# One core, a post-norm decoder layer: hand-written order lists for every engine from the last self-attention group to the first up products, key blocks zeroed by DMA, a new order of the start

## The reference, cut to what matters

```
x = layernorm(x + self_attention(x))      # 16 heads, low-rank q (384) and kv (128) latents, RMS norm, rope, causal
x = layernorm(x + cross_attention(x, ctx))# 16 heads of 32, keys and values from a 128-wide latent, causal
x = layernorm(x + ffn(x))                 # 2 shared experts (4096 hidden in all) and top 2 of 16 routed experts

q_c  = rms_norm(x @ wq_down.T) * q_norm_w ;  kv_c = rms_norm(x @ wkv_down.T) * kv_norm_w
k_rope = rope(x @ wk_rope.T)   # one rope key for all heads
scores = (q_nope k_nope + q_pe k_rope) / sqrt(192), causal; softmax; out = probs @ v ; out @ wo.T
```

## Time and profile before

| | |
|---|---|
| median of 3 runs | 903.31 us (902.88 to 906.53) |
| the profiled execution | 902.72 us, its span 900.9 us |
| PE busy | 838.2 us (93%) |
| PE weight loads busy | 710.2 us (79%) |
| DVE, ACT, POOL busy | 528.1, 474.8, 240.8 us |
| mean granted clock of PE | 0.988 |
| start up to the loop | 0 to 84.4 us |
| self-attention loop, 3 rounds | 84.4 to 301.1 us, 72.2 us a round |
| last self-attention group and the way into cross-attention | 301.1 to 391.5 us |
| cross-attention loop, 3 rounds | 391.5 to 489.3 us, 32.6 us a round |
| last cross-attention group and first up products | 489.3 to 521.5 us |
| feed-forward | 521.5 to 900.9 us |

### The profile page before, as it was taken

How to read it: one execution, slowest core, us unless ns; L and a number is a source line. 1 busy time by engine, 2 the same in 40 slices (tenths; PEclk the granted TensorE clock), 3 DMA queues, 4 the chain that set the end, 5 groups by cost and what they waited for, 6 DMA issues and landing times.

```text
span 900.9 us, 13299 instructions
## 1 busy us (share of the span) xinstructions
PE 838.2 (93%) x4302; PEld 710.2 (79%) x4302; DVE 528.1 (59%) x979; ACT 474.8 (53%) x1225; POOL 240.8 (27%) x278
## 2 busy tenths in 40 slices
PE   6978999999999987889998789999999999999997
PEld 5766888788788775777776678888888988889896
DVE  3553753654664557666767755636465665656467
ACT  5514752743753554676576651525473745637150
POOL 0222230132132021455455100431232332321420
PEclk9989999999999998999999999999999999999999
DMA  8022315133322400321222020543464564653432
GB/s 324 1 78 63 123 43 157 65 99 98 123 85 55 146 21 21 84 49 38 55 52 67 2 71 24 183 166 119 146 206 164 187 199 153 198 166 131 137 94 82
DMA packets 39486, 96.33 MB, mean 107 GB/s; under 512 B 15824, under 2 KB 21840, under 8 KB 37808
## 3 DMA queue, kind: packets, MB, share of 16 engines
q1 hardware_dynamic: 28384, 57.95, 20.6%
q0 software_dynamic: 11056, 37.79, 12.9%
HBM read 71.59 MB, written 20.97 MB: 103 GB/s over the span
## 4 chain that ended last, share of the span: by engine, by line
PE 62%; issue 15%; DVE 8%; ACT 7%; POOL 4%; SPq 1%; DMA 1%; POOLq 0%; ACTq 0%; DVEq 0%
PE ps L1490 50%; ACT Pt L829 3%; PE ps L1505 3%; PE ps L1830 2%; POOL Pt L593 2%; PE ps L1820 1%; PE ps L1550 1%; PE ps L1640 1%; DVE negmax L1101 1%; SPq L514 1%; DVE acc L1117 1%; PE ps L1711 1%; PE ps L1832 1%; DVE kb L1218 1%; DVE stats L1123 1%
## 5 line engine op out<-in xcount | busy, mean ns | idle before, releaser
L593 POOL TENSOR_TENSOR Pt<-Pt,rowinv 112x448 f32<-112x448 f32 x64 | 59.9, 936 | 226.6 <-DVE rowinv L1108 226.2
L829 ACT ACTIVATE Pt<-ps,negmax 112x112 f32<-112x112 f32 x256 | 87.2, 356 | 49.1 <-DVE negmax L1101 49.0
L1490 PE MATMUL ps<-x2T_hi,ws_hi 128*128 128x448 f32 x256 | 96.0, 375 | 4.3 <-DVE x2T_lo L1030 4.3
L1490 PE MATMUL ps<-x2T_lo,ws_hi 128*128 128x448 f32 x256 | 94.2, 368 | 0.0
L1490 PE MATMUL ps<-x2T_hi,ws_lo 128*128 128x448 f32 x256 | 94.1, 368 | 0.0
L1490 PE MATMUL ps<-w_hi,h_hi 128*128 128x512 f32 x224 | 89.9, 401 | 0.0
L957 ACT ACTIVATE hf<-ps,b 128x448 f32<-128x448 f32 x64 | 40.6, 635 | 92.3 <-PE ps L1490 72.9
L1490 PE MATMUL ps<-w_hi,h_lo 128*128 128x512 f32 x224 | 88.5, 395 | 0.0
L1490 PE MATMUL ps<-w_lo,h_hi 128*128 128x512 f32 x224 | 88.4, 395 | 0.0
L1030 DVE TENSOR_TENSOR h_lo<-hf,h_hi 128x448 fp32r<-128x448 f32 x64 | 39.9, 623 | 48.7 <-ACT h_hi L958 47.9
L1374 DVE TENSOR_TENSOR acc<-ps,acc 128x512 f32<-128x512 f32 x56 | 38.6, 689 | 44.4 <-PE ps L1490 35.4
(11 more groups left out here) (282 smaller groups left out, 2248.6 us busy)
## 6 DMA issues: line engine op xcount, KB each, us to landing
stage<-in_wf SPq DMA_DIRECT2D x30, 513.0 KB
rows_in<-in_zeros SPq DMA_DIRECT2D x30, 256.0 KB, 4.0
xs<-rows_in POOLq DMA_DIRECT2D x29, 256.0 KB, 4.3
rows_out<-yb POOLq DMA_DIRECT2D x29, 256.0 KB
stage<-in_wa SPq DMA_DIRECT2D x4, 1408.0 KB, 6.6
stage<-in_wb SPq DMA_DIRECT2D x4, 1280.0 KB, 5.6
qr<-ro_hi SPq DMA_DIRECT2D x64, 56.0 KB, 2.0
qr<-ro_lo SPq DMA_DIRECT2D x64, 56.0 KB, 2.0
```

The source lines that it names most:

```text
L593: nc.gpsimd.tensor_tensor(p, p, rowinv[0:S, b % 2, :].unsqueeze(2).broadcast_to([S, GH, S]), ALU.mult).then_inc(norm_done, 1)
L829: last = nc.scalar.activation(Pt[0:S, b % 2, h * S:(h + 1) * S], ps[0:S, b % 2, h * S:(h + 1) * S], ACT.Exp, bias=negmax[0:S, b % 2, h:h + 1],
L1490: ins = mm(dst, w, x, start=start and i == 0, stop=stop and i == len(ops) - 1, skip_group_check=not (start and stop))
```

## The change

1. The start. ACT loads the table for `Sqrt` before the data are there, and the additions of epsilon on DVE are gone (they are the bias of the square root). PE's first products over the first slice of features go in the order in which their parts arrive. The turned latents, the rope keys and the first `A`, `E`, `O` items are interleaved: PE does the first half's rope keys, then `A 0`, `A 1`, `E 0`, `O 0` in banks 2, 3, 0 and 1, then the second half's latents. The first `wa_lo` is made by DVE instead of POOL, and the rope keys are added and split by POOL instead of DVE and ACT.
2. `att_ready` and `x_ready` are gone; each of the first two bank users of a loop waits for its own bank.
3. The last self-attention group, the start, loop and last list of cross-attention are written item by item for each engine. `V 0` moves behind the first `Q`, one layer norm row moves from ACT to DVE, two of the four first splits of feed-forward weights (`F 2`, `F 3`) move on POOL from the start of cross-attention to its last group.
4. `kb` is zeroed by four transfers of 128x4x448 from a zeroed row `kz` instead of four DVE memsets; in the cross-attention loop SP spreads the first half's keys before it waits for the second part of the weights.

The diff, cut to its core:

```diff
-ROWS_ON_DVE = [2, 3]
+ROWS_ON_DVE = [2, 3, 6]
+ATT_PRE = _lat0 + [("KR", 0), ("A", 0), ("A", 1), ("E", 0), ("O", 0)] + _lat1 + [
+    ("KR", 1), ("A", 2), ("E", 1), ("O", 1), ("Q", 0, 0)] + _q
+ATT_PRE_DVE = _lat0 + [("RMS", 1), ("KR", 0), ("NAT", 1), ("A", 0), ("A", 1), ("E", 0), ("O", 0)] + _lat1 + [
+    ("KR", 1)] + _kvn + [("A", 2), ("E", 1), ("O", 1), ("Q", 0, 0)] + _q
+ATT_LAST_PE = [
...
+    ("W", 0), ("Z", 2), ("S", 4), ("T", 3), ("G", 6), ("W", 1), ("Z", 3), ("T", 4), ("G", 7), ("S", 5), ("S", 6),
+    ("Z", 4), ("W", 2), ("T", 5), ("W", 3), ("S", 7), ("Z", 5), ("T", 6), ("K", 0), ("Z", 6), ("W", 4), ("T", 7),
+    ("W", 5), ("Z", 7), ("U1", 0), ("U1", 1), ("U1", 2), ("U1", 3), ("W", 6)]
+X_PRE_PE = [
+    ("U1", 4), ("Q", 0), ("V", 0), ("U1", 5), ("S", 0), ("S", 1), ("U1", 6), ("K", 1), ("V", 1), ("S", 2), ("T", 0),
+    ("Q", 1), ("S", 3), ("T", 1), ("Z", 0), ("S", 4), ("T", 2)]
+X_PE = [
+    ("Z", 1), ("S", 5), ("T", 3), ("S", 6), ("Z", 2), (NEXT, "K", 0), ("Z", 3), ("T", 4), (NEXT, "Q", 0), ("S", 7),
+    ("T", 5), (NEXT, "V", 0), (NEXT, "S", 0), ("W", 0), ("Z", 4), ("Z", 5), ("W", 1), ("T", 6), (NEXT, "K", 1),
+    (NEXT, "S", 1), ("T", 7), (NEXT, "Q", 1), (NEXT, "S", 2), ("Z", 6), ("Z", 7), ("W", 2), (NEXT, "T", 0),
+    (NEXT, "S", 3), (NEXT, "T", 1), ("W", 3), (NEXT, "V", 1), (NEXT, "S", 4), ("W", 4), (NEXT, "Z", 0),
+    (NEXT, "T", 2), ("W", 5), ("W", 6)]
+X_LAST_PE = [
+    ("Z", 1), ("T", 3), ("S", 5), ("S", 6), ("Z", 2), ("T", 4), ("Z", 3), ("S", 7), ("W", 0), ("T", 5), ("Z", 4),
+    ("T", 6), ("Z", 5), ("W", 1), ("W", 2), ("W", 3), ("Z", 6), ("T", 7), ("Z", 7), ("U2", 0), ("U2", 1), ("U2", 2),
+    ("U2", 3), ("W", 4), ("W", 5), ("FF", 0), ("W", 6), ("FF", 1), ("FF", 2), ("FF", 3), ("U2", 4), ("U2", 5),
+    ("U2", 6)]
...
-            sp.wait_ge(kb_zero, 2)
+            sp.wait_ge(kz_set, 1)
+            sp.wait_ge(a_free["G"], NG * B)
+            for half in range(2):
+                for a in range(2):
+                    sp.dma_start(f32(kb[:, half, a, :, :, :]).rearrange("p b h s -> p b (h s)"),
+                                 f32(kz[:, :]).unsqueeze(1).broadcast_to([P, HB, GH * S])).then_inc(kb_zero[half], 16)
+            sp.wait_ge(kb_zero[0], 32)
             spread_keys(0, 0)
...
                 load_x(g, 0, X_O, xl_ld)
+                spread_keys(g, 0)
                 sp.wait_ge(xo_lo, g)
                 load_x(g, X_O, X_SIZE, xo_ld)
-                spread_keys(g, 0)
                 spread_keys(g, 1)
...
-            for i, (lo, hi) in enumerate(A_PIECES):
-                pool.wait_ge(a_hi, i + 1)
-                nc.gpsimd.tensor_tensor(wa_lo[:, lo:hi], stage[:, lo:hi], f32(wa_hi[:, lo:hi]),
-                                        ALU.subtract).then_inc(a_lo, 1)
...
+                elif kind == "KR":
+                    cols = slice(j * HALF, (j + 1) * HALF)
+                    rot = rope_keys[j]
+                    pool.wait_ge(kr_mul, j + 1)
+                    nc.gpsimd.tensor_tensor(rot[:, 0, :], rot[:, 0, :], rot[:, 1, :], ALU.add).then_inc(kr_rot, 1)
+                    pool.wait_ge(kr_rot, j + 1)
+                    nc.gpsimd.tensor_tensor(kr_hi[:, cols], rot[:, 0, :], one[:, :].broadcast_to([P, HALF]),
+                                            ALU.mult).then_inc(krh, 1)
+                    pool.wait_ge(krh, j + 1)
+                    nc.gpsimd.tensor_tensor(kr_lo[:, cols], rot[:, 0, :], f32(kr_hi[:, cols]), ALU.subtract)\
+                      .then_inc(krl, 1)
...
-            act.wait_ge(one_set, 1)
+            act.wait_ge(one_set, 3)
+            nc.scalar.activation(warm[:, :], one[:, :], ACT.Sqrt)
...
+            for i, (arrived, n) in enumerate(((in_hi, 2), (in_lo, 1), (in_lo, 2))):
+                pe.wait_ge(arrived, n)
+                for b in range(HB):
+                    mm(ps[0:S, b, :], *down_terms(b, 0)[i], start=i == 0, stop=False, skip_group_check=True)
```

More of the change, by code:

```diff
@@ L183 @@
[L183 to L191, removed]
@@ L238, in count, with first_after @@
         return self.per[item[0]] * g + self.rank[item] + 1
+    def first_after(self, places, item):
+        n = places.index(item)
+        return None if n > 1 else [i for m, i in enumerate(self.pre if places is self.body else self.last)
+                                   if m % 2 == n][-1]
     def base(self, g):
@@ L246, in place @@
         n = places.index(item)
-        if n >= 2:
+        if places is self.pre and item in PRE_BANK:
+            return Place(PRE_BANK[item] - 6, number + n, None, None)
+        if n >= 2 and places[n - 2] not in PRE_BANK:
             dg, prev = group_of(places[n - 2])
@@ L258, with turns @@
 Place = namedtuple("Place", "bank number prev prev_count")
-AJ = Jobs(0, ATT_PRE, ATT_PE, ATT_LAST_PE, "AEOQGBWKV")
+AJ = Jobs(0, ATT_PRE, ATT_PE, ATT_LAST_PE, "AEOQGBWK")
 XJ = Jobs(AJ.end, X_PRE_PE, X_PE, X_LAST_PE, "QKVW", X_DONE)
-def turns(fori, jobs, pre, body, last, step, between=None):
+def turns(fori, jobs, pre, body, last, step):
     def run(order, places, g, number):
@@ L773, in _, with squares @@
             copy(maskb[0:S, :], maskf[0:S, :]).then_inc(const_done, 1)
-            for r in range(2):
+            def squares(r):
                 for b in range(HB * r, HB * r + HB):
@@ L934, in x_step @@
                     turned(0, j, x1T_hi)
[L935 to L938 removed]
+                elif kind == "EXP":
+                    function_ready(ACT.Exp)
                 elif kind == "ROOT2":
@@ L1065, in _, with values @@
                     ins.then_inc(nat_done, 1)
-                for b in range(HB * r, HB * r + HB):
-                    dve.wait_ge(kvn_hi, b + 1)
-                    low(kvN_lo[0:S, b, :], nat[0:S, b % 4, QR:QR + LAT], kvN_hi[0:S, b, :])\
-                        .then_inc(kvn_lo, 1)
-                    dve.wait_ge(tr_hi, b + 1)
-                    cols = slice(b * S, (b + 1) * S)
-                    low(qkT_lo[:, :, cols], ps[:, b, 0:4 * S].rearrange("p (c s) -> p c s", c=4),
-                        qkT_hi[:, :, cols]).then_inc(tr_lo, 1)
+            def values(b):
+                dve.wait_ge(kvn_hi, b + 1)
+                low(kvN_lo[0:S, b, :], nat[0:S, b % 4, QR:QR + LAT], kvN_hi[0:S, b, :]).then_inc(kvn_lo, 1)
+            rms(0)
+            latents(0)
+            for i, (lo, hi) in enumerate(A_PIECES):
+                dve.wait_ge(a_hi, i + 1)
+                low(wa_lo[:, lo:hi], stage[:, lo:hi], wa_hi[:, lo:hi]).then_inc(a_lo, 1)
+            for b in range(HB):
+                values(b)
             def table(i):
@@ L1185, in att_step @@
                     ins.then_inc(a_free[kind], 1)
+                elif kind == "LAT":
+                    dve.wait_ge(tr_hi, j + 1)
+                    cols = slice(j * S, (j + 1) * S)
+                    low(qkT_lo[:, :, cols], ps[:, j, 0:4 * S].rearrange("p (c s) -> p c s", c=4),
+                        qkT_hi[:, :, cols]).then_inc(tr_lo, 1)
+                elif kind == "RMS":
+                    rms(j)
+                elif kind == "NAT":
+                    latents(j)
+                elif kind == "VAL":
+                    values(j)
+                elif kind == "KR":
+                    for s in range(2):
+                        dve.wait_ge(kr_done, 2 * j + s + 1)
+                        ins = nc.vector.tensor_tensor(batches(rope_keys[j][:, s, :]),
+                                                      batches(ps[:, 2 * j + s, 0:HALF]), table(2 + s), ALU.mult)
+                    ins.then_inc(kr_mul, 1)
                 elif kind == "SA":
@@ L1530, in _ @@
                         .then_inc(kr_done, 1)
-                if half == 0:
-                    for b in range(HB, B):
-                        turn_latents(b)
-            pe.wait_ge(tr_lo, B)
             def heads(ap):
```

250 lines of the change are left out of this document (129 added, 121 removed), and 43 rows, old and new, of tables (ATT_LAST_ACT, ATT_LAST_DVE, ATT_LAST_PE, X_LAST_ACT).

## The result

The changed kernel takes 858.75 us (median of 4 runs, 856.66 to 860.35) against 903.10 for the kernel before (4 runs, 902.07 to 906.53). The ratio is 0.9501, 95% interval 0.9469 to 0.9534. The forecast was 865 us, 850 to 881. The profiled execution took 858.94 us with a span of 857.1, so 43.8 us of span are gone. PE's idle time in the span fell from 62.7 to 30.1 us, and its busy time from 838.2 to 827.0 us with the same 4302 matmuls; the mean granted clock rose from 0.988 to 0.996.

A forecast was written before the change was run, and what follows sets the result against it. PE, busiest in every stage, was taken to bound the kernel, losing time idle or at the lower clock. Gains of 13.5 + 10.5 + 1.0 + 8.4 + 4.5 + 0.2 = 38.1 us off 902.72 gave 864.6, stated as 865, range 850 to 881.

The forecast's parts named there:

- the start: Start, up to the self-attention loop: waits and lower-clock time go, 13.5 us gained, between 10 and 16.
- the last group: Last cross-attention group: feed-forward products and W items cover layer norm and splits, 4.5 of 9.5 us gained, between 2 and 7.
- signs of being wrong: PE waiting for kb, kvN_lo taking 1 us or more with PE behind it, or second-loop rounds above 31.5 us.
- (f): Start: POOL's rope keys beside DVE's kvN_lo take 2 us of DVE and PE time away, bounds 0 and 3.5.
- (a): Start: table loaded before the data and PE beginning with hi*hi, 2.0 us gained, bounds 1.3 and 2.1.
- (d): Start: Q 1 1 no longer has to be split before the loop starts, 1.7 us gained.
- The last self-attention group: Last self-attention group: transfers replace DVE memsets and items are reordered, 10.5 us gained, between 7 and 14.
- The cross-attention loop: Cross-attention loop: new lists cover the small waits, 2.8 us a round, 8.4 in three, between 1.0 and 4.6 a round.
- slower than before: Rival: S 0 waits for keys in every cross-attention round and the clock falls, 908 us; chance 0.04.
- The way in: Stretch between self-attention and the cross-attention loop: half of its 2.0 us idle time kept, 1.0 us gained.
- Waits that only move: Rival: no gain in the cross-attention loop and half the last self-attention group's gain lost, 878 us; chance 0.22.
- All gaps closed: Rival: all PE idle time after its first matmul and the clock loss go, 54 us, 849; chance 0.13.

The follow-up runs named there:

- e11: Changed kernel without the early load of ACT's table, new order of first products kept; 858.75 us, ratio 0.9526.
- e10: Changed kernel with the four zeroing transfers of the key blocks issued three times over, each set after the last landed; 876.53 us, ratio 0.9718.
- e3: Changed kernel with the key blocks zeroed by four DVE memsets again and the zeroing transfers dropped; 866.64 us, ratio 0.9611.
- e2: Changed kernel, but in the cross-attention loop SP again spreads the first half's keys after waiting for the second part of the weights; 882.02 us, ratio 0.9782.
- e4: Changed kernel with U2 4 to U2 6 ahead of FF 3 on PE and ahead of FF 2 on ACT; 857.23 us, ratio 0.9508.
- e7: e4 with the gate's copies and first split of down weights taken out of FF 1 and put behind U2 on ACT and DVE; 853.14 us, ratio 0.9465.
- e8: e7 with W 4 ahead of Z 7 on PE, Z 5 ahead of SQRT on ACT, last self-attention group's W 0 behind Z 2 and S 4; 852.28 us.
- e12: e8 with SB 1 and G 1 swapped on ACT in self-attention; 852.73 us, ratio 0.9457.
- e6: The changed kernel itself, run again beside the kernel before; 858.01 us, ratio 0.9519.
- e9: Changed kernel with rope keys added and their low part made by DVE, high part copied by ACT, instead of POOL; 860.98 us, ratio 0.9554.

## Why the prediction was right, and where a size was off

**The mechanism and the sign** held: PE lost time in five stages, idle or at the lower clock level, and the new order takes most of it back; 43.8 us are gone where 38.1 were forecast. 32.6 of them are idle time. The terms did not all hold: the start passed its upper bound of 16 by 0.2, and the last group, by the estimate below, fell short of its lower bound of 2. One of the prediction's own signs of being wrong came in small: a `kvN_lo` took 1.25 us and PE waited 0.6 us behind it.

**The start.** The walk was right (`G 0` at 64.8 us, predicted 64.6; PE's first product at 5.0, predicted 4.8; granted clock 1.00). The sum was below it by the 2.0 us for DVE and POOL blocking each other (f). The blocking is real (`kvN_lo` 2.60 us for 0.9), but DVE was waiting for PE on both sides of it, and PE waited 0.6 for what DVE made next. The table's part of (a) is 1.0 to 1.5 us at the loop (e11), too little to be told in the whole time. (d), 1.7 us, was counted as gone: 1.1 of it moved into the first loop round. With the 1.5 us that the self-attention loop took longer, 14.7 us are left of the 16.2, nearer to the forecast than the row of the start shows.

**The last self-attention group.** 11.5 for 10.5; the waits found by the walk (0.6 us at `Z 6`) were there at 0.7. The price of the zeroing transfers was too high: 16 us taken from the earlier trace rows, 11.7 measured (e10), in both cases hidden. What I did not say is what the memsets would cost under the new lists: 8.3 us (e3). Without the transfers 2.6 us of that stage's gain are left.

**The cross-attention loop** is the term that was mis-sized most: 2.8 us a round taken, 4.1 measured, a round of 28.48 us with PE busy throughout. I had 27.8 us of products and left 2.0 of doubt on the chain from `K 0` to `S 0`; the chain (about 5.8 us in the trace, from the end of `K 0` near 387.9 to the landing at 393.7) did fit under the products, with nothing to spare. e2 shows that the doubt was at the right place: the rival "slower than before" named this wait with 3 us and 8.6 us of clock a round; with SP's old order the round pays 5.5 us and about 2 by the clock.

**The way in and the last group.** 5.3 gained together, 5.5 forecast, but that is luck: the way in gained more than its 1.0 and the last group less than its 4.5. The borders of the lists moved, so PE's idle time has to tell them apart. On the way in it went from 1.95 us to 0, and the granted clock from 0.92 over 20.8 us (1.7 us) to 1.00: I had put that stretch's clock loss with the stage before. In the last group it went only from 9.6 to 7.1 us, and about 1.3 of these 2.4 us were given back at the lower clock level (`U2 0` to `U2 3`, see the last section), so by this estimate it gained little more than 1 us. The half change (the wait ahead of `FF 4`) was priced at 1.4 us and cost 3.7, because the gate's copies and a split of weights stand in `FF 1` on ACT ahead of `x2T_hi` (e4, e7). The 2.2 us for the layer norm of the first tiles did not show ahead of `U2 0`; 2.1 us stood ahead of `Z 7` instead, and e8 shows that with them gone the layer norm's chain takes them back at `FF 0`. **The end:** the 0.17 us of the earlier trace rows do not show.

**The rivals.** Waits that only move were seen in small (`G 1`; `Z 7`; e12) but not in the loop. All gaps closed (849) was short by 10 us; e8, at 852, shows that 6 of them were two waits in the last groups (`FF 4` and `W 0`) with the clock behind them.

## What to carry to other kernels

When lists and a transfer queue are changed together, test each alone: here neither gained in the loop without the other, and the lists without SP's order were 24 us slower than with it. What an operation on a vector engine costs depends on the list around it: 7.5 us of memsets cost 8.3 here, while 1.7 us more for `kvN_lo` left a wait of 0.6, so price it with the new list. An item of a list can hold work that its name does not tell: walk the instructions and not the items.

## What the runs showed that was not expected

The same gap did not always lower the clock. PE waits 2.14 to 2.15 us ahead of `Z 7` in the changed kernel and in e7, with the same work ahead of it; then the 16 matmuls of `U2 0` to `U2 3` take 3.53 us in the one (456.96 to 460.49) and 2.24 in the other (456.44 to 458.68). The granted clock of these stretches, changed kernel and e7:

```profile
456.96:460.49 3.53, 3.48 (x17) 3.24 (x18) 2.28 (x5) 2.44 (x4) 3.08 (x4) 0.60 0.00 0
...
456.44:458.68 2.24, 2.18 (x17) 1.95 (x18) 1.59 (x4) 2.09 (x4) 1.86 (x3) 1.00 0.00 0
```

e3, e4, e6 and e11 are like the first, e9 like the second. It moves `FF 0` by 1.0 us; e12, whose waits there are as short as those of e8, has the slow form (3.63 us). What decides it stays open. A difference of about 1 us between two such kernels may come from that alone, as 1.0 of e7's 5.4 us did.
